# Sorting tokens for sixteen experts: from four-row groups of one tile to five-row groups of a pair of tiles

## The chip, the core and the metric

The kernel runs on one core of a Trainium2 chip. The metric is the device time of one execution, in microseconds (us). A time "before" or "after" is the median of several executions; one further execution of each kernel was profiled, and all durations below are from it.

## What is computed

`x` has shape (8, 64, 32, 32). A convolution-like block is added to it (a layer norm over channels, a projection to 16 channels, a Fourier filter, a projection back). Its result is read as 8192 tokens of 64 channels, and a mixture of experts is added:

```python
logits = einsum('bsd,de->bse', layernorm(t), gate_w) + gate_b   # 16 experts
top_probs, top_idx = top_k(softmax(logits), 2)                  # the best two of each token
dispatch = sum(one_hot(top_idx) * (top_probs / sum(top_probs))[..., None], axis=-2)
hidden = silu(einsum('bsd,edh->bseh', x, w1)) * einsum('bsd,edh->bseh', x, w2)
t = t + einsum('bseo,bse->bso', einsum('bseh,eho->bseo', hidden, w3), dispatch)
```

## The kernel before

The first 100 us (convolution block, gate logits of the first half) are the same in both kernels. The 8192 tokens are 64 tiles of 128 tokens, and two halves of 32 tiles (`HT`) that follow each other. Each half passes five stages.

1. **Route and sort.** VectorE picks the two best experts of each token (`route`) and works out each token's place in the tile, sorted by expert (`sort_places`). Each expert's tokens in a tile start at a multiple of `GRP` rows, so that a group of `GRP` rows belongs to one expert. For each tile VectorE builds a one-hot matrix in two instructions (`one_hots`, L1290 and L1292); TensorE multiplies by it (`sort_tile`, L872), once for each of the `GRP` rows of a group; ScalarE copies the sorted rows out of PSUM (`sorted_out`, L591 and L592); and GpSimd writes the tile's groups to `sorted_x` in HBM with one indirect transfer (`scatter`, L1479). TensorE also transposes the one-hots (`turn_hots`, L879) and ScalarE keeps them (`hott_out`, L599) for the way back.
2. **Load.** SyncE reads blocks of `GBLK` groups of one expert back (`load`), eight blocks (an octet) at a time. TensorE transposes them (L930), ScalarE copies them out (`tokens_out`, L618).
3. **Experts.** Four blocks are a quad `q`. For each quad TensorE runs the two up projections (`up`, L965 and L966, 16 matmuls, in high and low halves of float16), ScalarE the silu (`gate`, L624), VectorE the product (`product`, L1371), TensorE the down projection of quad `q - 2` (`down`, L978), ScalarE copies it out (`y_out`, L630) and SyncE stores it in `sorted_y` (`store_y`, L447). VectorE also copies each quad's weights to a fixed place (`fetch`, L1362), two quads ahead. L754 is a filler matmul that does no work.
4. **Return.** GpSimd gathers a tile's groups with one indirect transfer (`gather`, L1485). VectorE multiplies by the routing weights (`weigh`, L1378), ScalarE makes the high half (`high_part`, L636), VectorE the low half (`low_part`, L1384), and TensorE adds the rows back into token order (`back_to_tokens`, L992 to L1013).
5. **Result.** ScalarE copies out (`result`, L647) and SyncE stores.

The engines' order is written out by hand. The second half's sorting is spread over the first 19 quads of half 0 (`sorts_in`), and the first half's return over quads 4 to 21 of half 1 (`RET_START, RET_STEPS`). In half 1 a step of VectorE is `product(q)`, `fetch(q + 2)`, then for each tile `m` of the step `weigh(m)` and `low_part(m - 1)`. A step of TensorE is `up(q)`, `down(q - 2)`, an octet's transposes in every second step, and `back_to_tokens(m - BACK_LAG)`, with `BACK_LAG` 3. In half 1 the matmuls of the second up projection read their weights from `w_all` at an address in a register; the first reads the copy. The second half's return runs alone, after the last quad. 16 of its 32 transposed one-hots were kept; the others are built and transposed again there (`remade`).

```python
            def weigh(m):
                dve.wait_ge(gathered[m % YL_RING], 16 * (m // YL_RING + 1))
                ...
            def low_part(m):
                dve.wait_ge(yw_done, m + 1)
                dve.wait_ge(yhi_done, m + 1)
                ...
            def back_to_tokens(m):
                pe.wait_ge(ylo_done, m + 1)
```

Sizes follow from `GRP`: with 4, a tile has 76 groups (`TGROUPS`), a block 32 groups, a half 92 blocks and so 23 quads.

Of the kernel before, what the change touches and what calls it, by code (L numbers as in the profile page):

```python
# [10 lines left out]
I32 = mybir.dt.int32  # L11
# [24 lines left out]
GRP = 4  # L36
TGROUPS = (2 * P + E * (GRP - 1)) // GRP
TSLOTS = TGROUPS * GRP
GBLK = P // GRP
QUAD = 4  # L40
# [5 lines left out]
OROWS = OCT * P  # L46
# [18 lines left out]
HOTS = 6  # L65
SORT_RING = 8
# [3 lines left out]
PAST_AFTER, OWNERS_AFTER, ROUTE_AFTER = 8, 17, 14  # L70
COUNTS_AFTER, RANKS_AFTER, PLACES_AFTER = 24, 27, 29
UPFRONT, SORT_STEPS = 4, 19
FILLERS, HALF1_FILLED = 1, 6
EARLY_BASE = 3
KEPT = 16
XG_RING, YS_RING, YL_RING = 4, 8, 8
SPLIT_RING = 4
ACC_BANKS, HOTT_TAIL, OUT_BANKS = (4, 5), (0, 1), (2, 3)
ADD_LAG = 6
RET_START, RET_STEPS, BACK_LAG = 4, 18, 3  # L80
TURN = 4
RESULT_LAG = 5
OUT_AT = {2: 0, 5: 1, 8: 2, 11: 3}
# [52 lines left out]
def constant_tile():  # L136

    eye = np.eye(P)
    mean = np.kron(np.eye(2), np.full((C, C), 1.0 / C))
    rev = np.broadcast_to((E - np.arange(E))[None, :, None], (P, E, HT)).reshape(P, -1)  # L140
    lane = np.arange(P)[:, None]
# [22 lines left out]
def build(nc, x, w_in, w_out, bin_w, gate_w, gate_b, w1, w2, w3, t_const, t_perm, t_fwd, t_neg, t_inv, t_bins, out):  # L164
    ctx = ExitStack()
    with ctx:
# [3 lines left out]
        def sem(name):  # L170
# [41 lines left out]
        stepped_to = picked_space[0:TGROUPS, 0:E * HT]  # L212
        stepped = shared16[0:TGROUPS, after + 4 * PIX:after + 4 * PIX + 2 * E * HT].bitcast(F32)
# [9 lines left out]
        xg = w_raw16[:, 0:XG_RING * OROWS].rearrange("p (o n) -> p o n", n=OROWS)  # L223
# [48 lines left out]
        addr_f = sb("addr_f", [TGROUPS, HT])  # L272
        addr = sb("addr", [TGROUPS, HALVES, HT], I32)
        back_f, back = sb("back_f", [TGROUPS, HT]), sb("back", [TGROUPS, HALVES, HT], I32)
        hots = [tok[:, :, :, :].rearrange("p a t c -> p (a t c)").bitcast(F16)[:, r * TSLOTS:(r + 1) * TSLOTS].rearrange("p (g s) -> p g s", s=GRP)
                for r in range(HOTS)]
        sorted_t = [xs[:, :].bitcast(F16)[0:TGROUPS, r * BLK:(r + 1) * BLK] for r in range(SORT_RING)]
        yl = [xs[0:TGROUPS, COLS // 2 + r * GRP * C:COLS // 2 + (r + 1) * GRP * C] for r in range(YL_RING)]
        hott = [t[0:TGROUPS, r * BLK:(r + 1) * BLK].rearrange("g (s t) -> g s t", s=GRP)
                for t, n in ((xq.bitcast(F16), 16), (w_raw16[:, XG_RING * OROWS:], 12), (turned_space, 4)) for r in range(n)]  # L280
        kept_hott = [t[0:TGROUPS, r * BLK:(r + 1) * BLK].rearrange("g (s t) -> g s t", s=GRP)
                     for t, n in ((shared16, 8), (work[:, 4, :].bitcast(F16), 4), (picked_space.bitcast(F16), 4)) for r in range(n)]
        yw = [cand[:, :, :, :].rearrange("p k e t -> p (k e t)").bitcast(F32)[0:TGROUPS, r * GRP * C:(r + 1) * GRP * C].rearrange("g (s c) -> g s c", s=GRP)
              for r in range(2)]
        y_parts = [chosen[:, :, :, :, :].rearrange("p k j e t -> p (k j e t)")[0:TGROUPS, r * BLK:(r + 1) * BLK].rearrange("g (s a c) -> g s a c", s=GRP, a=2)
# [9 lines left out]
        sorted_y = [nc.dram_tensor(f"sorted_y{k}", (SLOT_BLOCKS * P, C), F32).ap() for k in range(HALVES)]  # L295
# [1234 lines left out]
```

## Time and profile before

| | |
|---|---|
| median of 3 runs | 378.61 us (377.3 to 378.87) |
| the profiled execution | 376.88 us |
| its span, first to last instruction | 374.8 us |
| busy: TensorE / VectorE / ScalarE / GpSimd | 298.6 / 268.9 / 221.5 / 179.5 us |
| mean granted clock of TensorE | 0.762 of 2.4 GHz |
| indirect transfers | 64 scatters and 64 gathers |

The profile gives for each instruction its start and duration, for each idle stretch what ended it, and TensorE's granted clock (1.0 is 2.4 GHz, 0.5 is 1.2 GHz). Matmuls overlap each other: their pace is the difference of two starts, not their duration. The five stages lie in time as follows: common start to 100.8, sorting of half 0 to 162.6, quads of half 0 to 233.7, quads of half 1 to 311.2, and from the first gather of half 1's return at 318.1 to the end.

### The profile page before, as it was taken

To read this page: it belongs to the slowest core of one execution; us is meant where nothing else is said; L and a number is where in the kernel's file an instruction comes from. 1 tells how busy PE (TensorE), PEld (TensorE's weight loads), DVE (VectorE), ACT (ScalarE), POOL (GpSimd) and SP (SyncE) were. 2 spreads that over 40 slices of the span, in tenths; PEclk is the share of its full clock that TensorE was granted. 3 is DMA by queue.
4 is the path that set the end of the run, shared out by engine and by line. 5 is a ranking of instruction groups with operands and counts; after the bars stand their busy time and mean duration, and the time that the engine had idled before them with its cause. 6 is when DMAs were issued, how large, how long until landed. Compare 5 with 4: busy or idle time off the path is not lost.

```text
span 374.8 us, 8710 instructions
## 1 busy us (share of the span) xinstructions
PE 298.6 (80%) x2802; PEld 251.6 (67%) x2802; DVE 268.9 (72%) x716; ACT 221.5 (59%) x484; POOL 179.5 (48%) x157
## 2 busy tenths in 40 slices
PE   4879567957476677469999998998878895799996
PEld 4737346855255554259998987888777784588884
DVE  1964574497999954959999967467878885883762
ACT  4878844562177675449898985455555552555431
POOL 2016263330088785445655650077865400887880
PEclk9959985555855568659999999898999996555555
DMA  7999900000012121242545454455544512233432
GB/s 222 338 260 385 387 24 0 2 2 0 0 45 53 50 56 35 65 118 47 137 117 139 114 133 90 99 138 142 132 106 107 128 37 53 50 103 87 111 79 70
DMA packets 55390, 39.89 MB, mean 106 GB/s; under 512 B 37660, under 2 KB 49692, under 8 KB 54708
## 3 DMA queue, kind: packets, MB, share of 16 engines
q1 hardware_dynamic: 42804, 29.25, 27.5%
q0 software_dynamic: 12384, 10.10, 11.3%
q8 instruction: 24, 0.39, 0.5%
q14 instruction: 18, 0.15, 0.1%
q10 hardware_dynamic: 160, 0.01, 0.0%
HBM read 20.08 MB, written 19.14 MB: 105 GB/s over the span
## 4 chain that ended last, share of the span: by engine, by line
PE 36%; DVE 26%; ACT 11%; issue 10%; DMA 8%; POOL 4%; SPq 2%; DVEq 1%; POOLq 0%; ACTq 0%
PE banks L978 7%; PE banks L872 4%; DMA w_raw<-in_L_ffn_w 4%; POOL xs L1485 4%; PE banks L966 4%; PE banks L965 4%; DVE tok L1292 4%; DMA xs<-sorted_y,back 3%; DVE cand L1378 3%; PE banks L879 3%; PE banks L930 3%; PE banks L1013 2%; PE banks L764 2%; ACT fold L624 2%; DVE work L1362 2%
## 5 line engine op out<-in xcount | busy, mean ns | idle before, releaser
L1479 POOL DMA_INDIRECT sorted_x<-xs,addr x64 | 75.7, 1183 | 67.4 <-ACT xs L591 36.5
L1485 POOL DMA_INDIRECT xs<-sorted_y,back x64 | 74.7, 1167 | 65.0 <-issue 53.6
L591 ACT CAST xs<-banks 76x512 f16<-76x512 f32 x64 | 37.2, 581 | 34.7 <-PE banks L872 34.5
L636 ACT CAST chosen<-cand 76x256 f16<-76x256 f32 x64 | 25.9, 405 | 49.6 <-DVE cand L1378 37.1
L978 PE MATMUL banks<-w_all,power 128*128 x368 | 51.4, 285 | 4.3 <-DVE power L1371 2.3
L872 PE MATMUL banks<-shared,tok 128*76 128x131 f16 x256 | 34.8, 274 | 23.9 <-ACT wcol L592 13.3
L978 PEld LDWEIGHTS banks<-w_all,power 128*128 128x128 f32 x368 | 47.0, 199 | 6.0 <-issue 5.6
L1371 DVE SCALAR_TENSOR_TENSOR power<-banks,fold 128x512 f32<-128x512 f32 x46 | 31.7, 688 | 25.2 <-ACT fold L624 21.7
L872 PEld LDWEIGHTS banks<-shared,tok 128*76 128x76 f16 x256 | 25.7, 167 | 31.1 <-DVE tok L1292 19.9
L1292 DVE SCALAR_TENSOR_TENSOR tok<-perm,local,tok 128x304 f16<-128x304 f16 x80 | 42.7, 534 | 2.8
L1362 DVE COPY work<-w_all 128x512 uint16 (+1 forms) x184 | 39.1, 282 | 6.6 <-issue 6.3
L879 PE MATMUL banks<-ident,tok 128*76 128x128 f16 x256 | 36.5, 286 | 4.5 <-DVE tok L1292 2.6
L965 PE MATMUL banks<-shared,work 128*128 128x128 f16 x276 | 37.3, 224 | 0.0
L966 PE MATMUL banks<-shared,work 128*128 128x128 f16 x276 | 37.3, 224 | 0.0
L1378 DVE TENSOR_TENSOR cand<-xs,w_loc 76x256 f32<-76x256 f32 x64 | 26.9, 420 | 9.7 <-DMA xs<-sorted_y,back 6.6
L879 PEld LDWEIGHTS banks<-ident,tok 128*76 128x76 f16 x256 | 28.4, 174 | 7.4 <-ACT scratch L599 4.0
L1384 DVE TENSOR_TENSOR chosen<-cand,chosen 76x256 f16<-76x256 f32 x64 | 26.7, 417 | 7.9 <-ACT chosen L636 7.9
L966 PEld LDWEIGHTS banks<-shared,work 128*128 128x128 f16 x276 | 27.8, 101 | 3.7 <-issue 0.6
L624 ACT ACTIVATE fold<-banks 128x512 f32<-128x512 f32 x46 | 27.4, 596 | 4.1 <-PE banks L966 3.6
L618 ACT COPY shared<-banks 128x1024 f16<-128x1024 f16 (+1 forms) x24 | 23.4, 974 | 8.1 <-PE banks L930 7.8
L1290 DVE TENSOR_SCALAR tok<-perm,local 128x304 f16<-128x304 f16 x80 | 25.3, 317 | 3.8 <-PE banks L879 3.8
L965 PEld LDWEIGHTS banks<-shared,work 128*128 128x128 f16 x276 | 27.7, 100 | 0.0
(200 smaller groups left out, 620.0 us busy)
## 6 DMA issues: line engine op xcount, KB each, us to landing
sorted_x<-zeros SPq DMA_DIRECT2D x2, 2944.0 KB, 30.4
w_raw<-sorted_x SPq DMA_DIRECT2D x22, 256.0 KB, 3.5
sorted_y<-filt SPq DMA_DIRECT2D x96, 32.0 KB
sorted_y<-enh SPq DMA_DIRECT2D x88, 32.0 KB
w_raw<-in_L_ffn_w SPq DMA_DIRECT2D x5, 512.0 KB, 16.1
xs<-in_x SPq DMA_DIRECT2D x8, 256.0 KB, 4.6
out<-cen_sq SPq DMA_DIRECT2D x8, 256.0 KB, 3.7
shared<-in_t_fwd SPq DMA_DIRECT2D x1, 1024.0 KB, 7.8
```

The costliest lines, as they stand in the source:

```text
L591: nc.scalar.copy(sorted_t[n % SORT_RING].rearrange("g (a b n) -> g a b n", a=2, b=2), sorted_rows[:, :, :, 0:2 * C]).then_inc(sorted_done, 1)
L624: nc.scalar.activation(gated[:, q % 2, :], bank[q % 2], ACT.Silu, scale=1.0 / WSCALE).then_inc(silu_done, 1)
L872: last = nc.tensor.matmul(banks[SORT_PAIR][0:TGROUPS, s // 2, at:at + ROW], hots[n % HOTS][:, :, s], rows[:, n, 0:ROW], start=True, stop=True)
L879: last = nc.tensor.transpose(target.bitcast(F16)[0:TGROUPS, s * P:(s + 1) * P], hots[use % HOTS][:, :, s], ident16[:, :])
L965: nc.tensor.matmul(dst, up_weights(k, i, b, a, experts), tokens[:, b, :, :], start=True, stop=False)
L966: last = nc.tensor.matmul(dst, up_weights(k, i, b, a + 1, experts), tokens[:, b, :, :], start=False, stop=True)
L978: last = nc.tensor.matmul(y_bank(q)[:, b * C:(b + 1) * C], hid[:, q % RING, b * P:(b + 1) * P], of_expert(experts[(q % NQ % 2) * QUAD + b] ...
L1292: nc.vector.scalar_tensor_tensor(hot, slot_iota, local[:, k, 0, t:t + 1], hot, ALU.is_equal, ALU.add).then_inc(hot_done, 1)
L1362: last = nc.vector.tensor_copy(fetched_w[:, (q % FETCH_RING) * QUAD + b, 0:parts_read * HID], w_all[:, bass.ds(fetching[o][(i % 2) * QUAD ...
L1378: nc.vector.tensor_tensor(yw[m % 2], yl[m % YL_RING].rearrange("g (s c) -> g s c", s=GRP), w_loc[:, k, t, :].unsqueeze(2).to_broadcast([TG ...
L1479: nc.gpsimd.indirect_dma_start(out=sorted_x[k].rearrange("(g s) c -> g (s c)", s=GRP), out_offset=bass.IndirectOffsetOnAxis(ap=addr[:, k, ...
L1485: nc.gpsimd.indirect_dma_start(out=yl[m % YL_RING], out_offset=None, in_=sorted_y[k].rearrange("(g s) c -> g (s c)", s=GRP), in_offset=bas ...
```

## The change

`GRP` becomes 5. A tile then has 64 groups, so that two tiles (a pair) fill 128 partitions: a half has 16 pairs (`HP`), and every sort, scatter, gather and return handles a pair. A block is 25 groups (125 rows), a half has 100 blocks and 25 quads. There are 32 scatters and 32 gathers, of 128 rows of 1280 bytes, in place of 64 and 64 of 76 rows of 1024 bytes. All 32 transposed pairs of one-hots are kept, so nothing is remade. The sort's PSUM pair is used as two halves in turn (rows 0 to 2, rows 3 and 4 of a group). `fetch` copies all four parts of the weights in half 1 too. `store_y` is one transfer of 125 partitions instead of four of 32, and `load` reads 100 partitions instead of 128. `weigh` works in place, on 128 partitions; `high_part` and `low_part` work on each tile's 64 partitions apart, into `y_parts`, which GpSimd zeroes once. `back_to_tokens` first adds the residual and the means, then waits, then runs 10 matmuls of 128 by 128. `BACK_LAG` becomes 1. The results of the first half go straight from PSUM, during half 1.

```diff
-GRP = 4
+GRP = 5
-RET_START, RET_STEPS, BACK_LAG = 4, 18, 3
+RET_START, RET_STEPS, BACK_LAG = 4, 18, 1
...
             def store_y(q):
                 k, i = q // NQ, q % NQ
-                rows = sorted_y[k][i * BLK:(i + 1) * BLK, :].rearrange("(b g s) c -> s g b c", b=QUAD, s=GRP)
                 sp.wait_ge(y_done, q + 1)
-                for s in range(GRP):
-                    sp.dma_start(rows[s], ys[q % YS_RING][s * GBLK:(s + 1) * GBLK, :].rearrange("g (b c) -> g b c", b=QUAD)).then_inc(y_stored[q % YS_RING], 16)
+                sp.dma_start(sorted_y[k][i * QW:(i + 1) * QW, :].rearrange("(b p) c -> p b c", p=BW),
+                             ys[q % YS_RING][0:BW, :].rearrange("p (b c) -> p b c", b=QUAD)).then_inc(y_stored[q % YS_RING], 16)
...
             def high_part(m):
+                act.wait_ge(parts_zero, 1)
                 act.wait_ge(yw_done, m + 1)
                 if m >= SPLIT_RING:
                     act.wait_ge(back_ps, m - SPLIT_RING + 1)
-                nc.scalar.copy(y_parts[m % SPLIT_RING][:, :, 0, :], yw[m % 2]).then_inc(yhi_done, 1)
+                for h in range(2):
+                    nc.scalar.copy(y_parts[m % SPLIT_RING][tile_half(h), :, 0, h, :], yl[m % YL_RING][tile_half(h), :, :]).then_inc(yhi_done, 1)
...
+            def sort_pair(n, a):
+                k, j = n // HP, n % HP
+                for h in range(2):
+                    pe.wait_ge(hot_done, 2 * n + h + 1)
+                if j == 0 and a == 0:
+                    pe.wait_ge(mean1_done, 1)
+                    pe.wait_ge(wt_done, k + 1)
                 if n >= 1:
-                    pe.wait_ge(wcol_done, n)
+                    pe.wait_ge(wcol_done, 2 * n + a - 1)
+                for s in rows_in(a):
+                    at = (s - rows_in(a)[0]) * ROW_STRIDE
+                    for h in range(2):
+                        hot = hots[n % HOTS][:, h * TSLOTS:(h + 1) * TSLOTS].rearrange("p (g s) -> p g s", s=GRP)
+                        last = nc.tensor.matmul(banks[SORT_PAIR][tile_half(h), a, at:at + ROW], hot[:, :, s], rows[:, 2 * n + h, 0:ROW], start=True, stop=True)
+                last.then_inc(sort_ps, 1)
...
             def back_to_tokens(m):
 
-                pe.wait_ge(ylo_done, m + 1)
...
+                n, u = m // BP, m % BP
+                sums = bank[ACC_BANKS[n % 2]][:, u * P:(u + 1) * P]
+                if u == 0 and n >= 2:
+                    pe.wait_ge(res_done, n - 1)
+                nc.tensor.matmul(sums, ct[:, m, 0:P], ident, start=True, stop=False)
+                for h in range(2):
+                    nc.tensor.matmul(sums[h * C:(h + 1) * C, :], both_parts[:, 2 * m + h:2 * m + h + 1].to_broadcast([P, C]), mean_rows[:, :],
+                                     start=False, stop=False)
+                pe.wait_ge(hott_done, m + 1)
+                pe.wait_ge(ylo_done, 2 * (m + 1))
                 for s in range(GRP):
                     for a in range(2):
-                        last = nc.tensor.matmul(acc[h * C:(h + 1) * C, u * P:(u + 1) * P], y_parts[m % SPLIT_RING][:, s, a, :], home[:, s, :],
-                                                start=False, stop=(s == GRP - 1 and a == 1))
+                        last = nc.tensor.matmul(sums, y_parts[m % SPLIT_RING][:, s, a, :, :], hott[m][:, s, :], start=False, stop=(s == GRP - 1 and a == 1))
                 last.then_inc(back_ps, 1)
...
             def return_step(m):
-                k, t = m // HT, m % HT
                 weigh(m)
-                if t >= 1:
+                if m >= 1:
                     low_part(m - 1)
```

TensorE in half 1, between two quads, before: the end of a down projection (L978), one tile's return (L992, L995) and the next up projection (L965). Bracketed are the semaphores that a row waits for.

```order
L978 MATMUL banks<-w_all,power 128x64
L992 MATMUL banks<-ident,mean_rows 128x128 [waits hott_done,ylo_done]
L995 MATMUL banks<-chosen,scratch 128x128 x4
L965 MATMUL banks<-shared,work 128x128 [waits silu_done,fetched,xt_done]
L966 MATMUL banks<-shared,work 128x128
```

The same place in the changed program, for a pair (L983, L985 and L991 are its return, L960 the next up projection):

```order
L973 MATMUL banks<-w_all,power 125x64
L983 MATMUL banks<-cst,ct 128x128
L985 MATMUL banks<-mean_rows,both_parts 64x128 x2
L991 MATMUL banks<-w_raw,xs 128x128 [waits ylo_done,hott_done]
L991 MATMUL banks<-w_raw,xs 128x128 x9
L960 MATMUL banks<-shared,work 128x125 [waits silu_done,fetched,xt_done]
```

The place of the return between `down` and the next `up` is the same; the wait for the low parts has moved behind the residual and means, and it is now for pair `m - 1` of the step, not for tile `m - 3`.

VectorE in half 1, one step before: the copies of weights (L1362, each with a row that sets its address), then `weigh` (L1378), `low_part` (L1384), the sums of four tiles (L1390, L1391), a second tile, and the next quad's product (L1371).

```order
L1362 COPY work<-w_all 128x256
L1378 TENSOR_TENSOR cand<-xs,w_loc 76x256 [waits ylo_done,gathered6]
L1384 TENSOR_TENSOR chosen<-cand,chosen 76x4x64 [waits yhi_done,yw_done]
L1390 TENSOR_TENSOR ct<-ct,banks 128x2x128 [waits back_ps]
L1391 TENSOR_TENSOR ct<-ct,banks 128x2x128 [waits dve_own]
L1378 TENSOR_TENSOR cand<-xs,w_loc 76x256 [waits ylo_done,gathered7]
L1384 TENSOR_TENSOR chosen<-cand,chosen 76x4x64 [waits yhi_done,yw_done]
L1371 SCALAR_TENSOR_TENSOR power<-banks,fold 128x512 [waits y_ps,h2_done,silu_done]
```

The changed program's step (L1315 copies weights, L1328 weighs pair `m`, L1335 makes the low parts of pair `m - 1`, L1324 is the next product):

```order
L1315 COPY work<-w_all 128x512
L1315 ISA
L1315 COPY work<-w_all 128x512
L1328 TENSOR_TENSOR xs<-xs,w_loc 128x320 [waits gathered3]
L1335 TENSOR_TENSOR xs<-xs 64x5x64 [waits yhi_done] x2
L1324 SCALAR_TENSOR_TENSOR power<-banks,fold 128x500 [waits y_ps,h2_done,silu_done]
```

The low parts that TensorE waits for in a step stand behind the four weight copies and `weigh` of the same step, which themselves stand behind that step's product.

## Rows read from the trace of the kernel before

**Rows 1.** Busy time by stretch: us, each engine's busy time (instructions), clock, DMA.

```profile
100.80:162.60 61.80, 40.63 (x306) 30.59 (x307) 50.41 (x124) 40.30 (x107) 41.22 (x35) 0.58 0.23 61
162.60:233.70 71.10, 66.98 (x836) 62.33 (x837) 59.32 (x180) 57.47 (x129) 34.50 (x30) 0.95 0.44 105
233.70:311.20 77.50, 66.14 (x795) 60.64 (x795) 55.61 (x184) 41.49 (x90) 36.78 (x32) 0.96 0.47 110
318.10:374.80 56.70, 50.45 (x395) 40.69 (x393) 34.96 (x91) 24.78 (x56) 37.94 (x32) 0.50 0.30 83
```

**Rows 2.** Chain that ended last, in the sorting of half 0: start, us, what.

```profile
130.30 0.65 PE banks L872 x4
130.97 0.45 ACT xs L591
131.45 0.17 ACT wcol L592
131.76 0.65 PE banks L872 x4
```

**Rows 3.** Timeline of VectorE, one tile's one-hots and the next's.

```profile
108.30 0.28 DVE L1290 TENSOR_SCALAR tok<-perm,local 128x304 f16<-128x304 f16 x1
109.07 0.29 DVE L1290 TENSOR_SCALAR tok<-perm,local 128x304 f16<-128x304 f16 x1
```

**Rows 4.** Timeline of VectorE in half 0: four weight copies, then a one-hot.

```profile
216.05 0.90 DVE L1362 COPY work<-w_all 128x512 uint16 x4 [0.25 <-issue]
216.87 0.29 DVE L1290 TENSOR_SCALAR tok<-perm,local 128x304 f16<-128x304 f16 x1
```

**Rows 5.** Timelines of TensorE, ScalarE and VectorE, early quads of half 1.

```profile
237.75 0.38 PE L754 MATMUL banks<-perm,ident 128*128 128x512 f16 x1
239.76 0.38 PE L754 MATMUL banks<-perm,ident 128*128 128x512 f16 x1
...
242.86 0.38 PE L754 MATMUL banks<-perm,ident 128*128 128x512 f16 x1
...
240.62 0.60 ACT L624 ACTIVATE fold<-banks 128x512 f32<-128x512 f32 x1 [0.28 <-PE banks L966]
...
241.25 0.69 DVE L1371 SCALAR_TENSOR_TENSOR power<-banks,fold 128x512 f32<-128x512 f32 x1 [0.46 <-ACT fold L624]
```

**Rows 6.** Timeline of TensorE in half 1: five matmuls lie between these two starts.

```profile
267.59 0.22 PE L992 MATMUL banks<-ident,mean_rows 128*128 128x128 f16 x1
...
267.87 0.22 PE L992 MATMUL banks<-ident,mean_rows 128*128 128x128 f16 x1
```

**Rows 7.** Groups of the page: busy us, mean ns of one, idle before.

```profile
L1479 POOL DMA_INDIRECT sorted_x<-xs,addr x64 | 75.7, 1183 | 67.4 <-ACT xs L591 36.5
L1485 POOL DMA_INDIRECT xs<-sorted_y,back x64 | 74.7, 1167 | 65.0 <-issue 53.6
...
L1378 DVE TENSOR_TENSOR cand<-xs,w_loc 76x256 f32<-76x256 f32 x64 | 26.9, 420 | 9.7 <-DMA xs<-sorted_y,back 6.6
```

**Rows 8.** TensorE by stretches of 2 us in half 1: busy time, granted clock, DMA.

```profile
256.00:258.00 2.00, 0.98 (x15) 1.00 0.52 118
258.00:260.00 2.00, 2.00 (x19) 0.50 0.36 72
```

**Rows 9.** End of the chain that ended last.

```profile
364.36 4.14 DMA xs<-sorted_y,back
...
369.33 0.79 PE banks L1007 x2
...
370.37 1.30 PE banks L1013 x16
```

**Rows 10.** Busy time by stretch, in half 0 and in half 1 with stores alone.

```profile
186.00:216.00 30.00, 29.40 (x383) 27.78 (x381) 27.89 (x81) 27.27 (x63) 17.38 (x15) 1.00 0.53 127
302.00:310.00 8.00, 7.00 (x83) 6.29 (x82) 6.58 (x20) 4.19 (x11) 0.00 (x0) 1.00 0.20 41
```

More of the change, by code:

```diff
@@ L278, in build @@
[L278 to L282, printed above, removed]
@@ L454, in _ @@
                     store_y(NQ * k + 2 * o + h)
+                    if k == 1 and 2 * o + h in STORE_AFTER:
+                        store(STORE_AFTER[2 * o + h])
                 if n + XG_RING < HALVES * OCTETS:
                     load(n + XG_RING)
-            for n in range(NBLK):
+            for n in range(len(STORE_AFTER), NBLK):
                 store(n)
@@ L868, in sort_tile @@
                 if n >= 1:
-                    pe.wait_ge(wcol_done, n)
-                for s in range(GRP):
-                    at = (s % 2) * ROW_STRIDE
-                    last = nc.tensor.matmul(banks[SORT_PAIR][0:TGROUPS, s // 2, at:at + ROW], hots[n % HOTS][:, :, s], rows[:, n, 0:ROW], start=True, stop=True)
-                last.then_inc(sort_ps, 1)
-            def turn_hots(use, target):
-                pe.wait_ge(hot_done, use + 1)
-                for s in range(GRP):
-                    last = nc.tensor.transpose(target.bitcast(F16)[0:TGROUPS, s * P:(s + 1) * P], hots[use % HOTS][:, :, s], ident16[:, :])
+                    pe.wait_ge(wcol_done, 2 * n + a - 1)
@@ new lines, in sort_places, with one_hots @@
+                step(nc.vector.scalar_tensor_tensor(back_f[:, :], addr_f[:, :], lane, bank[MISC_BANK][:, P:P + HT], ALU.add, ALU.add))
+                for h in range(2):
+                    nc.vector.tensor_copy(addr[tile_half(h), k, :], tiles_of(back_f, h)).then_inc(addr_done, 1)
+                for h in range(2):
+                    nc.vector.tensor_scalar(back[tile_half(h), k, :], tiles_of(back_f, h), SLOT_GROUPS - 1.0, None, ALU.min).then_inc(addr_done, 1)
+            def one_hots(n):
+                k, j = n // HP, n % HP
+                if n >= HOTS:
+                    dve.wait_ge(hott_ps, n - HOTS + 1)
+                hot = [hots[n % HOTS][:, h * TSLOTS:(h + 1) * TSLOTS] for h in range(2)]
+                for h in range(2):
+                    nc.vector.tensor_scalar(hot[h], slot_iota, local[:, k, 1, 2 * j + h:2 * j + h + 1], None, ALU.is_equal).then_inc(hot_second, 1)
+                for h in range(2):
+                    dve.wait_ge(hot_second, 2 * n + h + 1)
+                    nc.vector.scalar_tensor_tensor(hot[h], slot_iota, local[:, k, 0, 2 * j + h:2 * j + h + 1], hot[h], ALU.is_equal, ALU.add).then_inc(hot_done, 1)
@@ L1294, in experts_of_groups @@
             def experts_of_groups(k):
-                nc.vector.tensor_reduce(group_expert[:, k, :], stepped.rearrange("p (e t) -> p t e", e=E), AX_X, ALU.add)
+                step(nc.vector.tensor_reduce(group_of[:, :], stepped.rearrange("p (e t) -> p t e", e=E), AX_X, ALU.add))
+                for h in range(2):
+                    nc.vector.tensor_copy(group_expert[tile_half(h), k, :], tiles_of(group_of, h))
             def slot_weights(k):
```

453 lines of the change are left out of this document (183 added, 270 removed).

## The prediction

> **What bounds the kernel now.** I read the busy times by stretch first, then in each stretch the chain of waits or the timelines of the engines that wait for each other. No engine bounds the whole program: each stretch has its own limit.
>
> In the sorting of half 0, 61.8 us, no engine is busy throughout and TensorE's clock is mostly the lower one [rows 1]. The chain shows a closed circle of one tile: four sort matmuls, ScalarE's copies of the rows and of the weight columns, the next tile's four matmuls, 1.46 us from start to start [rows 2]. TensorE has one PSUM pair for it and waits until it is empty. VectorE alone would make a tile's one-hots in 0.77 us [rows 3].
>
> In half 0, TensorE, VectorE and ScalarE are all over 90% busy at the full clock in the 30 us from 186 to 216 [rows 10]. Nothing there can be added for nothing.
>
> In half 1, 77.5 us for 23 quads or 3.37 each, TensorE is 85% and VectorE 72% busy [rows 1]. The limit is order, not work.
>
> The last stretch, 56.7 us, holds half 1's return alone, at a clock of 0.50 [rows 1]. GpSimd issues a gather each 1.47 us (1.167 and a gap of 0.3) [rows 7]. From the first gather at 318.1 to the last at 364.36 [rows 1, 9] are 31 intervals of 1.49, so this pace sets the stretch. 10.4 us follow: landing, weighing, matmuls, result and store [rows 9].
>
> **The change part by part.**
>
> *Sorting of half 0.* The two PSUM halves in turn break the circle. A pair then costs each engine its own work. VectorE: twice 0.77, or 1.54 [rows 3]; 5% more columns, but two instructions no longer wait for their own results, so 1.5. ScalarE: copies of 1280 columns in place of 2048, about 1.4. TensorE at the lower clock: five transposes of 0.11 and ten sort matmuls of 64 output columns; a matmul of 128 columns takes 0.056 at full clock (five in 0.28 [rows 6]), so 0.11 at half, and the pair takes 1.65 if none of them overlap. I take 1.6 a pair, against 2.92. The first 14 tiles lie beside VectorE's routing of half 1 and give nothing. The other 18 take 26.3 now and nine pairs would take 14.4, which is 11.9 less. Of this I give back 3: the counts, ranks and places of half 1 stand among the last four pairs, and TensorE comes to them before VectorE is through with its one-hots. **−9 us**; bounds −4 (the routing's chain hides most) and −12.
>
> *Quads of half 0.* Each half has 25 quads, not 23. A quad without sorting takes 2.0 us, or 3.1 with an octet's transposes, so 2.55 in the mean (fillers at 237.75, 239.76, 242.86 [rows 5]). Now 71.1 us go to 23 quads [rows 1]. A quad with a pair will be held by VectorE: product 0.6, copies 0.82 [rows 4] and 0.13 for reading addresses, one-hots 1.5, so 3.05, which with three engines so full I round to 3.2. 14 such, 11 others at 2.3 to 2.5 and the slow first quads (71.1 less 19 at 3.05 and 4 at 2.3: 4) give 74. **+3**; bounds −3 and +7.
>
> *Quads of half 1.* This is where I expect the loss. In the new order, a step's low parts (pair `m - 1`) stand on VectorE behind its product, four copies and `weigh(m)`. TensorE waits for them before `up(q + 1)`, and the product of `q + 1` waits for that. So the engines close a circle in each step with a pair. From the start of `up`: silu 0.64 later (240.62 less 239.76 and 0.22 of filler), product 0.63 later, 0.6 of product [rows 5]; copies with addresses 0.95 [rows 4]; weighing and two low parts, each 0.42 by the row of 256 columns [rows 7] and 0.07 for 64 more, overlapping by 0.07 twice, 1.33; release 0.06; ten matmuls 0.56 [rows 6]. Sum 4.8 us. TensorE's other work (`down`, transposes, residual) lies in its shadow. Before, three tiles of lag kept the low parts a step ahead. There are 15 such steps. The other ten are five of 2.55 before the return, the first pair's at 3.2, one of 2.6 and three of 2.3, the last of which ends with its product, so two count. With 1.5 up to the first product: 72 + 12.8 + 3.2 + 2.6 + 4.6 + 1.5 = 96.7, against 77.5: +19. TensorE idles 1.7 of 4.8 us in it. Its clock fell at 258 after a stretch only half busy [rows 8], so I add 2 for such falls. **+21**; bounds: 0 if the circle does not close and VectorE or TensorE's own work of 3.1 decides, +34 if the lower clock stays (5.7 a step).
>
> The copies of all four parts cost VectorE 0.28 more a quad, which is in the circle. Their gain, no addresses in registers for the up projections, I put at nothing: TensorE does not wait for them in the circle.
>
> *The return of half 1.* 16 gathers for 32. The trace has none of 128 rows. If the cost is one of the instruction, the pace is 1.47; if it goes with rows, 1.47 × 128/76 = 2.5 at most. I take 1.7, nearer the first: scatters and gathers, which read and write different sides, cost nearly the same (1.183 and 1.167), so most of it looks like the instruction's own. Then 15 × 1.7 to the last gather, and behind it some 10.1 (half copies cost 0.9 more, the residual ahead of the wait saves 1.3): 35.6, against 56.7. But TensorE at the lower clock needs 0.8 for the residual [rows 9], 0.1 for the means and ten times 0.11, 2.0 a pair: 6.9 to its first matmul, 32 for 16 pairs, 3.1 behind, 42. Its clock may be up for part of it, since it would then work without a pause. I take 38.6 us. **−18**; bounds −25 (pace 1.47, full clock) and −9 (2.5).
>
> The four issues of the last store become one, which saves 1.3 us, and a longer landing takes it back. GpSimd's zeroing lies between its last scatter and first gather, where it idles. Storing three results in half 1 costs nothing: each waits for a result some quads old.
>
> *Sum.* −9 + 3 + 21 − 18 = −3, from the profiled 376.9 to 374. The median of the runs is 1.7 above that execution, so **376 us**.
>
> **The rivals.**
>
> *The forecast's mechanism*, gains at both ends and the circle in half 1, between 366 and 384: chance 0.50.
>
> *The circle does not close (faster).* If VectorE's low parts come so early that TensorE never waits, 15 steps cost 3.4 and not 4.8: 21 us less, 355. For it: TensorE's `down` and transposes fill 2 us of the wait. Against it: the rows put the low parts 4.2 us behind the start of `up`, and this decides from a lead of 1.4 on. 0.15.
>
> *The clock falls in half 1 (slower).* The same circle, with TensorE at 1.2 GHz: 0.45 more to the silu and 0.55 more for the return, 5.7 a step, 14 us more: 388. For it: the fall at 258. Against it: half-busy stretches elsewhere in half 1 kept the mean at 0.96 [rows 1]. 0.12.
>
> *Stores on few DMA engines (slower).* A store of 125 partitions has the same bytes as before, but may not spread as evenly. With stores alone, engines are 20% busy at 41 GB/s, so one full engine moves 13 GB/s in such rows; with loads and scatters beside them 15 [rows 10]. If only 5 of 16 engines carry a store of 128 KB, each is busy 2 us a quad with it, 0.85 with its part of loads on 10 engines and 0.5 with scatters, 3.3 in all, more than the 2.95 that a quad of half 0 takes: 8 us more, 384. Against it: eight store buffers and four load buffers take up waits. 0.13.
>
> The Trainium skill, "DMA: Bandwidth & Descriptors", section "Why a DMA increments its semaphore by 16 and not by 1", states this as a rule: a transfer uses the largest number of engines up to 16 that divides its slowest dimension, which it says gives 10 for 100 partitions. By it 125 gives 5. It would give 384 where even spreading gives 376, and no row here has a transfer of such a shape. By it the zero fill of `sorted_x`, also on 125 partitions, would take three times as long, into a part of the program in which nothing waits for it yet.
>
> *Gathers by rows (slower).* At 2.5 a gather, the last stretch gives back 9: 385. 0.10.
>
> **How the numbers follow.** The range from 361 to 392 holds the forecast's band, half of the faster case and most of the three slower ones, which leave out about 0.15 together. About 0.5% is what a measurement of this kernel can tell: 376.7 and 380.5. Faster: the 0.15 and two thirds of the forecast's 0.50, 0.48. Same: 0.12, all of it from the forecast's band. Slower: 0.35 from the last three rivals and 0.05 from the band's upper end, 0.40. Gains and losses of some 20 us nearly cancel, so the sign rests on which term I mis-sized.
>
> **What would show it.** In the profile of the changed kernel: sorts of half 0 at 1.6 us a pair, with quads starting near 153.5; 25 quads of half 0 in 74 us, with VectorE over 90% busy; steps of 4.8 us in half 1, with TensorE waiting for VectorE's low parts some 1.7 us in each of 15 steps; gathers each 1.7 us and a last stretch of 38 to 39. Steps of 3.4, a last stretch paced by 2.5, or long waits for loads and stores in half 0 would each prove a term wrong.

## The result, and the profile after

| | before | after |
|---|---|---|
| median of 4 runs each, us | 378.7 | 384.4 |
| profiled execution, us (its span) | 376.9 (374.8) | 383.7 (381.9) |
| granted clock, mean | 0.762 | 0.817 |

The ratio is 1.0145, with a 95% interval from 1.0114 to 1.0177: the changed kernel is slower by about 1.5%. The forecast was 376.0, faster by a little. Its range held the time, its sign was wrong. Below, a ratio leaves out an execution that took over 1.5% more than the fastest of its kernel, and a time is the median of all of them.

The stretches of the changed kernel, cut at the same events as [rows 1]: first sort matmuls, first token transposes, first `up` of half 1, last product, first gather of half 1's return. The columns are the same.

```profile
102.90:155.40 52.50, 30.01 (x304) 19.88 (x305) 47.63 (x129) 28.20 (x93) 20.52 (x18) 0.63 0.21 74
155.40:233.80 78.40, 74.22 (x955) 65.45 (x956) 58.63 (x187) 57.14 (x145) 17.91 (x17) 0.97 0.37 104
...
233.80:342.20 108.40, 82.15 (x935) 77.41 (x935) 56.16 (x163) 52.07 (x108) 15.26 (x16) 0.86 0.31 84
342.20:349.90 7.70, 2.19 (x19) 1.80 (x17) 0.67 (x1) 0.77 (x2) 0.00 (x0) 0.90 0.36 92
...
349.90:381.90 32.00, 21.05 (x234) 17.11 (x234) 23.05 (x50) 17.53 (x37) 16.83 (x16) 0.86 0.41 124
```

Set beside [rows 1], the terms of the sum come out so:

| stretch | forecast | measured |
|---|---|---|
| up to the first sort | 0 | +2.1 |
| sorting of half 0 (61.8 to 52.5) | −9 | −9.3 |
| quads of half 0 (71.1 to 78.4) | +3 | +7.3 |
| quads of half 1 (77.5 to 108.4) | +21 | +30.9 |
| last product to first gather (6.9 to 7.7) | 0 | +0.8 |
| return of half 1 (56.7 to 32.0) | −18 | −24.7 |
| sum | −3 | +7.1 |

Both large terms are of the kind that was forecast, and both are larger. Half 1 missed by 10 us and half 0 by 4; the return missed by 7 the other way. With half 1 as forecast and all else as measured, the sum would be −3.

**Half 1, step by step.** VectorE's timeline over two steps with a pair (start, us, what; in brackets the idle time before, and who ended it):

```profile
258.41 0.68 DVE L1324 SCALAR_TENSOR_TENSOR power<-banks,fold 128x500 f32<-128x500 f32 x1 [3.15 <-ACT fold L624]
259.01 0.89 DVE L1315 COPY work<-w_all 128x512 uint16 x4
259.81 0.48 DVE L1328 TENSOR_TENSOR xs<-xs,w_loc 128x320 f32<-128x320 f32 x1
260.22 1.00 DVE L1335 TENSOR_TENSOR xs<-xs 64x320 f16<-64x320 f32 x2
263.18 0.68 DVE L1324 SCALAR_TENSOR_TENSOR power<-banks,fold 128x500 f32<-128x500 f32 x1 [1.97 <-ACT fold L624]
264.17 0.90 DVE L1315 COPY work<-w_all 128x512 uint16 x4 [0.30 <-issue]
264.98 0.48 DVE L1328 TENSOR_TENSOR xs<-xs,w_loc 128x320 f32<-128x320 f32 x1
265.38 1.00 DVE L1335 TENSOR_TENSOR xs<-xs 64x320 f16<-64x320 f32 x2
269.53 0.68 DVE L1324 SCALAR_TENSOR_TENSOR power<-banks,fold 128x500 f32<-128x500 f32 x1 [3.15 <-ACT fold L624]
```

TensorE's matmuls of the return, which wait for the low parts, in the step before and in the same two steps, and ScalarE's silus behind them:

```profile
255.41 1.23 PE L991 MATMUL banks<-scratch,xs 128*128 128x128 f16 x10 [2.80 <-DVE xs L1335]
...
261.36 0.72 PE L991 MATMUL banks<-scratch,xs 128*128 128x128 f16 x10 [1.02 <-DVE xs L1335]
...
266.53 1.23 PE L991 MATMUL banks<-scratch,xs 128*128 128x128 f16 x10 [1.77 <-DVE xs L1335]
...
262.56 0.59 ACT L624 ACTIVATE fold<-banks 128x500 f32<-128x500 f32 x1 [1.24 <-PE banks L961]
...
268.63 0.59 ACT L624 ACTIVATE fold<-banks 128x500 f32<-128x500 f32 x1 [2.15 <-PE banks L961]
```

The first step is the circle of the forecast at full clock. From one product to the next: 0.60 of product, 0.80 of copies, 0.41 of weighing, 1.14 of low parts and release (TensorE starts at 261.36), 0.56 for ten matmuls, 0.64 to the silu, 0.62 to the product: 4.77, where 4.8 was forecast. In the second step the ten matmuls and the `up` run at 1.2 GHz: 1.02, 1.08 and 0.90 in those three places, 1.18 more. Another 0.39 goes to reading the addresses of a new octet before the copies. That makes 6.35. With and without the low clock and the reading, a step is 4.8, 5.2, 5.9 or 6.3 long. Twelve of the 15 steps in which TensorE returns a pair are within 0.1 of one of these, six of them at 5.9 or more; the other three take 5.0 to 5.4. Together they take 82.7 us, 5.5 each. In the first slow one, from 252 to 256, TensorE was busy 1.2 us of 4; its clock was 0.60 there and 0.54 in the next four:

```profile
252.00:256.00 4.00, 1.20 (x14) 0.97 (x12) 2.86 (x8) 2.16 (x6) 0.46 (x1) 0.60 0.47 129
256.00:260.00 4.00, 4.00 (x32) 3.98 (x30) 1.59 (x6) 0.66 (x2) 0.48 (x1) 0.54 0.17 44
```

### The profile page after: what moved, and what is told of

It is laid out like the page before. It is cut to its first block and busy times, and to the rows that moved or that the text cites. A ratio compares the mean times of both kernels' runs of the same rounds, so it can differ in the third digit from the quotient of the medians.

```text
span 381.9 us, 8236 instructions
## 1 busy us (share of the span) xinstructions
PE 280.9 (74%) x2886; PEld 236.0 (62%) x2886; DVE 252.4 (66%) x664; ACT 212.2 (56%) x486; POOL 99.6 (26%) x96
## 5 line engine op out<-in xcount | busy, mean ns | idle before, releaser
L1324 DVE SCALAR_TENSOR_TENSOR power<-banks,fold 128x500 f32<-128x500 f32 x50 | 33.8, 676 | 62.7 <-ACT fold L624 58.1
L1417 POOL DMA_INDIRECT xs<-sorted_y,back x32 | 32.1, 1003 | 115.0 <-DMA sorted_y<-filt 59.7
L1411 POOL DMA_INDIRECT sorted_x<-xs,addr x32 | 34.9, 1091 | 100.7 <-ACT xs L591 98.9
L961 PE MATMUL banks<-shared,work 128*128 128x125 f16 x400 | 56.6, 232 | 0.0
L960 PE MATMUL banks<-shared,work 128*128 128x125 f16 x400 | 56.5, 234 | 0.0
L973 PE MATMUL banks<-w_all,power 128*125 x400 | 56.1, 287 | 0.2 <-DVE power L1324 0.2
L1315 DVE COPY work<-w_all 128x512 uint16 x200 | 47.2, 298 | 9.0 <-issue 9.0
L973 PEld LDWEIGHTS banks<-w_all,power 128*125 128x125 f32 x400 | 51.4, 202 | 1.2 <-issue 0.3
L624 ACT ACTIVATE fold<-banks 128x500 f32<-128x500 f32 x50 | 29.9, 598 | 28.4 <-PE banks L961 27.9
L960 PEld LDWEIGHTS banks<-shared,work 128*128 128x128 f16 x400 | 42.3, 106 | 0.0
L871 PE MATMUL banks<-shared,tok 128*64 128x131 f16 x320 | 24.7, 284 | 19.5 <-DVE tok L1243 19.2
L1243 DVE SCALAR_TENSOR_TENSOR tok<-perm,local,tok 128x320 f16<-128x320 f16 x64 | 32.0, 539 | 0.0
L1335 DVE TENSOR_TENSOR xs<-xs 64x320 f16<-64x320 f32 x64 | 31.0, 484 | 1.0
L991 PE MATMUL banks<-scratch,xs 128*128 128x128 f16 x120 | 11.0, 253 | 18.2 <-DVE xs L1335 18.1
L1328 DVE TENSOR_TENSOR xs<-xs,w_loc 128x320 f32<-128x320 f32 x32 | 15.6, 488 | 11.3 <-DMA xs<-sorted_y,back 10.9
L991 PEld LDWEIGHTS banks<-scratch,xs 128*128 128x128 f16 x120 | 8.8, 113 | 19.5 <-issue 19.5
```

Source lines behind the costliest of these rows:

```text
L624: nc.scalar.activation(gated[:, q % 2, 0:QW], bank[q % 2][:, 0:QW], ACT.Silu, scale=1.0 / WSCALE).then_inc(silu_done, 1)
L871: last = nc.tensor.matmul(banks[SORT_PAIR][tile_half(h), a, at:at + ROW], hot[:, :, s], rows[:, 2 * n + h, 0:ROW], start=True, stop=True)
L960: nc.tensor.matmul(dst, up_weights(k, i, b, a, experts), tokens[:, b, :], start=True, stop=False)
L961: last = nc.tensor.matmul(dst, up_weights(k, i, b, a + 1, experts), tokens[:, b, :], start=False, stop=True)
L973: last = nc.tensor.matmul(y_bank(q)[0:BW, b * C:(b + 1) * C], hid[:, q % RING, b * BW:(b + 1) * BW], of_expert(experts[(q % NQ % 2) * QUAD ...
L1243: nc.vector.scalar_tensor_tensor(hot[h], slot_iota, local[:, k, 0, 2 * j + h:2 * j + h + 1], hot[h], ALU.is_equal, ALU.add).then_inc(hot_d ...
```

## The experiments

**1. A longer lag.** The circle needs the low parts of pair `m - 1` in the step that makes them. With a lag of 2, TensorE takes those that were written a step earlier.

```diff
-RET_START, RET_STEPS, BACK_LAG = 4, 18, 1
-RESULT_LAG = 2
+RET_START, RET_STEPS, BACK_LAG = 4, 18, 2
+RESULT_LAG = 3
```

> The changed kernel with BACK_LAG 2 (and RESULT_LAG 3, so that a result is asked for as late as before): TensorE does pair m - 2 where it did m - 1. Theory of the circle: the low parts of m - 2 were written a step earlier, so TensorE no longer waits 1.0 to 2.8 us a step for them, a step with a pair costs 3.5 to 3.9 us in place of 4.8 at full clock and 6.3 at the low one, and the low clock goes too because TensorE has no pauses: 20 to 28 us less, 356 to 364. Rival, the stretch is held by transfers (stores of 125 partitions, gathers behind them): the wait moves to the gathers and the time stays within 3 of 384. Rival, VectorE's work: steps of 4.4 or more, 376 or more.

Measured: 359.6 us, ratio to before 0.950 (0.946 to 0.953). From half 1's first product to its last it takes 82.4 us, against 106.9 in the changed kernel and 75.5 in the kernel before. Most steps with a pair alternate between 3.5 and 4.0, and the clock is 0.95 from 252 to 316. Two take 6.2 and 5.1; in the first of them TensorE waited 1.4 us for ScalarE and 1.1 for nothing that the profile names, and its clock was 0.50 from 282 to 288. So the circle was the cause of the loss: opening it gave back 25 us, where the rival of transfers had the time stay within 3.

**2. The same circle, shortened.** The lag stays at 1, but in half 1 VectorE weighs and writes the low parts ahead of its copies.

```diff
                     product(q)
+                    if k == 1:
+                        if i == 0:
+                            dve.wait_ge(wloc_done, HALVES)
+                        for m in pairs_in(i, RET_START, RET_STEPS):
+                            return_step(m)
                     if q + FETCH_AHEAD < HALVES * NQ:
                         fetch(q + FETCH_AHEAD)
...
-                    else:
-                        if i == 0:
-                            dve.wait_ge(wloc_done, HALVES)
-                        for m in pairs_in(i, RET_START, RET_STEPS):
-                            return_step(m)
```

> The changed kernel with VectorE's order turned in half 1: product, weighing and low parts, then the four copies. Theory of the circle: the 0.9 us of copies leave it, so each of 15 steps costs 3.9 us and not 4.8 at full clock: 13 less; where the lower clock goes away too, up to 9 more: 362 to 371. Rival, the copies were needed just as soon (TensorE then waits for them): within 3 of 384. Rival of transfers: no change either.

Measured: 360.3 us, ratio 0.952 (0.948 to 0.956). The timeline of one step, VectorE and TensorE:

```profile
263.47 0.68 DVE L1324 SCALAR_TENSOR_TENSOR power<-banks,fold 128x500 f32<-128x500 f32 x1 [0.97 <-ACT fold L624]
...
264.06 0.48 DVE L1328 TENSOR_TENSOR xs<-xs,w_loc 128x320 f32<-128x320 f32 x1
...
264.46 1.00 DVE L1335 TENSOR_TENSOR xs<-xs 64x320 f16<-64x320 f32 x2
...
265.49 0.97 DVE L1315 COPY work<-w_all 128x512 uint16 x4
265.61 0.72 PE L991 MATMUL banks<-scratch,xs 128*128 128x128 f16 x10 [1.02 <-DVE xs L1335]
...
269.56 0.72 PE L991 MATMUL banks<-scratch,xs 128*128 128x128 f16 x10 [0.56 <-DVE xs L1335]
```

The circle is still closed: TensorE waits for the low parts in 14 of the 15 steps, mostly 0.56 and 1.02 in turn and twice 1.35 and 1.48. But 13 of the steps are 3.95 or 3.96 long, 0.8 less than 4.77, the copies. And none is at the low clock: the granted clock is 1.00 from 252 to 316. So waits of 0.4 to 1.5 in steps of 4.0 kept the clock here, and waits of 1.0 to 2.8 in the changed kernel did not always.

**3. Fewer copies.** One part of the change is undone in half 1: `fetch` copies 256 columns in place of 512, and `up` reads w2's weights from `w_all` with addresses in registers.

```diff
-                return fetched_w[:, ((NQ * k + i) % FETCH_RING) * QUAD + b, a * HID:(a + 1) * HID].bitcast(F16)
+                if k == 0 or a < 2:
+                    return fetched_w[:, ((NQ * k + i) % FETCH_RING) * QUAD + b, a * HID:(a + 1) * HID].bitcast(F16)
+                return of_expert(experts[(i % 2) * QUAD + b], a, HID).bitcast(F16)
...
+                width = (4 if k == 0 else 2) * HID
...
```

> The changed kernel with one part of the change undone: in half 1 VectorE copies only the weights of w1, and w2's up matmuls read w_all through registers. Theory of the circle: four copies take 0.45 us less in it, 24 quads, 15 in the circle: 7 less, 377, if registers cost TensorE nothing. Rival, the addresses in registers cost TensorE time (half a microsecond a quad): within 3 of 384 or up to 6 slower. If VectorE's copies are not in the limit at all: no change.

Measured: 379.9 us, ratio 1.002 (0.998 to 1.006), 4.4 less than the changed kernel; half 1 takes 103.7 from product to product, 3.3 less. Its ten executions lie between 375.6 and 382.2. The direction is the circle's; the size is about half to two thirds of the 7 us that it gives.

**4 and 5. The clock.** First a filler matmul ahead of every `up`; then four of them in a step with a pair, ahead of the wait for the low parts.

```diff
-FILLERS, HALF1_FILLED = 1, 6
+FILLERS, HALF1_FILLED = 1, 25
```

> The changed kernel with HALF1_FILLED 25: a filler matmul of 512 columns ahead of every up, in half 1 too. It costs 0.22 us at full clock and stands in the circle: 19 quads, 4 more. Theory that part of the loss is the clock: with fewer half-idle stretches the nine steps of 6.3 us become 5.0, 12 less, net 8 less: 376. Rival, the clock falls all the same, since one filler fills little of 1.0 to 1.8 idle: 4 to 7 slower, 388 to 391.

```diff
                         if m >= BACK_LAG:
+                            pe.wait_ge(silu_done, q)
+                            stay_warm(4, bank[(q + 1) % 2])
                             back_to_tokens(m - BACK_LAG)
```

> The changed kernel with four filler matmuls of 512 columns (0.22 us each at full clock) issued in each step of half 1 with a pair, ahead of the wait for the low parts, so that they fill the pause and not the circle. Theory that the pauses of 1.0 to 1.8 us cost the clock, and that six of the 15 steps were 1.4 us longer for it: all 15 at 4.8 to 5.2, 6 to 10 us less, 374 to 378. Rival, the clock falls all the same: the fillers at the low clock take 1.7 us, and the time is 384 or more.

Measured: 388.9 (ratio 1.019, 1.013 to 1.025) and 375.5 (0.992, 0.989 to 0.996). The first kernel's executions took 385.0, 387.0, 390.7 and 394.2, and the profile is of the third; the changed kernel's took 383.7 to 384.9. TensorE in half 1 by stretches, first with a filler ahead of every `up`, then the changed kernel, then with four in the pause (columns as in [rows 1]):

```profile
252.00:340.00 88.00, 66.26 (x632) 59.68 (x633) 40.80 (x118) 36.82 (x76) 9.41 (x10) 0.77 0.25 69
```

```profile
252.00:340.00 88.00, 64.00 (x697) 60.31 (x694) 45.76 (x131) 40.54 (x85) 9.45 (x10) 0.83 0.27 73
```

```profile
252.00:333.00 81.00, 65.70 (x766) 56.29 (x766) 45.95 (x131) 41.57 (x87) 9.45 (x10) 0.98 0.30 81
```

The filler ahead of `up` stands behind the wait: it leaves the pause, and it is in the circle, whose shortest steps are 4.98 and not 4.77. The clock did not go up. It was 0.77 here against 0.83, but over whole executions it was 0.81 to 0.83 against 0.80 to 0.82, so that it went down is not shown. The expectation of 8 us less was wrong, and its rival, 4 to 7 more, came true. Four fillers in the pause cost the circle nothing. The clock is 0.98, and 12 of the 15 steps are at 4.77 or 5.17; one of 5.4 reads its addresses for longer, and the first two, 5.6 and 4.9, have the one fall of the clock that is left (0.50 from 258 to 260, behind a wait of 2.2). Together the 15 take 75.4 us and not 82.7. So the low clock cost the changed kernel at least 7 us in these steps.

**6. The lag alone, in the kernel before.**

```diff
-RET_START, RET_STEPS, BACK_LAG = 4, 18, 3
+RET_START, RET_STEPS, BACK_LAG = 4, 18, 1
```

> The kernel before with BACK_LAG 1 in place of 3 and nothing else. Theory that the lag alone closes the circle: product 0.6, copies 0.82, weighing and low parts of two tiles, release, eight matmuls, up and silu make 4.8 us a step in place of 3.37: 15 to 25 us more than 378.7, 394 to 404, all of it in half 1. Rival, the circle needs the pairs (128 rows weighed and split at once) and does not close on single tiles: within 3 of 378.7.

Measured: 416.7 us, ratio 1.096 (1.087 to 1.104), 38 more than before. Half 1 takes 112.5 from product to product and not 75.5, and between 240 and 350 TensorE waits for low parts 23 times, 17.0 us in all. Its row shows what came on top of the 15 to 25 us that were expected:

```profile
250.00:348.00 98.00, 80.85 (x625) 74.23 (x626) 49.36 (x157) 34.95 (x75) 32.33 (x29) 0.56 0.30 69
```

The clock is 0.56, where half 1 before had 0.96 [rows 1]: here the circle and the low clock come together in most steps. The circle does not need the pairs: the one number `BACK_LAG` closes it.

**7. Stores over more DMA engines.** A store of 125 partitions becomes one of 112 and one of 13.

```diff
-                sp.dma_start(sorted_y[k][i * QW:(i + 1) * QW, :].rearrange("(b p) c -> p b c", p=BW),
-                             ys[q % YS_RING][0:BW, :].rearrange("p (b c) -> p b c", b=QUAD)).then_inc(y_stored[q % YS_RING], 16)
+                for part in (slice(0, 112), slice(112, BW)):
+                    sp.dma_start(sorted_y[k][i * QW:(i + 1) * QW, :].rearrange("(b p) c -> p b c", p=BW)[part],
+                                 ys[q % YS_RING][part, :].rearrange("p (b c) -> p b c", b=QUAD)).then_inc(y_stored[q % YS_RING], 16)
...
```

> The changed kernel with each store of a quad's results in two transfers, one of 112 partitions and one of 13, in place of one of 125. Rival of the prediction (one transfer of 125 partitions goes over few DMA engines and its lateness holds quads or gathers): 3 to 8 us less than 384.4, most of it in half 0 (78.4 us) and in the landing of the last store, 4.7 us. Theory that the stores are hidden: within 2 of 384.4, with the landing of the last store alone shorter by up to 2 us.

Measured: 382.2 us, ratio 1.013 (1.007 to 1.019), whose interval overlaps that of the changed kernel. The last store in the chain that ended last, in the changed kernel and with the split:

```profile
344.59 4.61 DMA sorted_y<-filt
```

```profile
343.91 1.72 DMA sorted_y<-filt
```

This landing is 2.9 us shorter, and the last stretch waits for it. Half 0 is not shorter: 71.1 us from first to last product, against 71.0. The rival was right that such a store lands late and wrong on what it would hold up.

**8. What a gather costs.** An extra gather of 64 rows goes into spare buffers ahead of each gather of 128.

```diff
+                if m >= 3:
+                    pool.wait_ge(gathered[(m - 3) % YL_RING], 32 * ((m - 3) // YL_RING + 1))
+                nc.gpsimd.indirect_dma_start(
+                    out=again[m % 3], out_offset=None, in_=sorted_y[k].rearrange("(g s) c -> g (s c)", s=GRP),
+                    in_offset=bass.IndirectOffsetOnAxis(ap=back[tile_half(0), k, j:j + 1], axis=0)).then_inc(gathered[m % YL_RING], 16)
...
```

> The changed kernel with an extra gather of 64 rows into spare buffers ahead of each gather of 128 rows; the output is the same. If a gather costs by its rows, the extra one takes 0.5 us of GpSimd where the other takes 1.0; if it costs by the instruction, both take 0.9 to 1.1. The last stretch then has two instructions a pair: with rows 2.1 us a pair and 10 us more than 32.0, by the instruction 2.6 a pair and 18 us more.

Measured: 403.6 us in a single run. GpSimd's timeline in the last stretch, extra gathers (L1420) and the others (L1423):

```profile
353.39 0.90 POOL L1420 DMA_INDIRECT chosen<-sorted_y,back  x1 [0.30 <-issue]
354.60 0.95 POOL L1423 DMA_INDIRECT xs<-sorted_y,back  x1 [0.30 <-issue]
355.86 0.90 POOL L1420 DMA_INDIRECT chosen<-sorted_y,back  x1 [0.30 <-issue]
```

64 rows take 0.90 and 128 rows 0.95; over the 16 of each in this stretch the means are 0.97 and 0.99. The cost is the instruction's. The stretch from first gather to end is 50.9 us and not 32.0, 18.9 more where 18 were expected.

**9 to 12. A version that beats both.** Lag 2 and the early low parts together; then without fillers as well; then with the split stores; then with w2's weights read through registers again.

The edit of the second step:

```diff
-FILLERS, HALF1_FILLED = 1, 6
+FILLERS, HALF1_FILLED = 0, 6
```

> Both measures together: BACK_LAG 2, and VectorE weighs and writes the low parts ahead of its copies. With either alone half 1 took 3.7 to 4.0 us a step. If each took away another part of the circle, the sum is a step of 3.5, TensorE's own work, and 4 to 8 us less than either: 352 to 356. Rival, the circle is open with either and another one holds both at 3.5 to 4.0 (product, weighing, ScalarE's high parts, the next silu): within 3 of 360.

> The same with FILLERS 0: no filler matmul of 0.39 us ahead of the up projections of half 0 and of the first six quads of half 1. Theory that TensorE's own work holds the quads of half 0 (busy 29.9 of 30.0 us from 186 to 216): 31 fillers of 0.22 to 0.39 go, 6 to 11 less than with them. Rival, they fill only what TensorE would wait for VectorE's products (the forecast's view of half 0): no change, or slower where the clock falls without them.

> BACK_LAG 2, low parts ahead of the copies, no fillers, and each store of results in two transfers, of 112 and of 13 partitions. In the changed kernel the split took the landing of the last store from 4.6 to 1.7 us. If that is all that the stores cost: 3 less than 348.8, 346. Rival, with steps of 2.9 us the slow stores now hold back more than the last one: 5 or more less, under 344. Rival, two issues a quad cost what they save: 348 to 350.

> The same kernel, and in half 1 VectorE copies only w1's weights, w2's up matmuls reading w_all through registers as in the kernel before. Theory that VectorE's own work holds the open steps (product 0.6, weighing 0.4, low parts 0.95, copies 0.95: 2.9): they fall to 2.45, 15 of them, 7 to 10 us less. Rival, TensorE's own work holds them (and the reading of addresses adds to it): no gain, or up to 8 us more.

| kernel | median, us | ratio to before (95%) | half 1, first to last product | clock there |
|---|---|---|---|---|
| both | 350.5 | 0.925 (0.923 to 0.927) | 71.7 | 1.00 |
| and no fillers | 348.8 | 0.919 (0.916 to 0.923) | 73.3 | 0.97 |
| and split stores | 341.5 | 0.901 (0.896 to 0.906) | 71.8 | 0.97 |
| and half the copies | 346.4 | 0.915 (0.911 to 0.919) | 75.7 | 0.98 |

Together they take eight of the 15 steps with a pair in 2.8 to 2.9, where each alone took 3.5 to 4.0, so the expected floor of 3.5 for TensorE was too high. To leave the fillers out gave 1.7 us, where 6 to 11 were expected. In half 1 of the third of these kernels TensorE hardly pauses any more, and in the fourth it pauses more although VectorE has less to do:

```profile
252.00:302.00 50.00, 48.77 (x668) 45.77 (x665) 44.66 (x129) 38.90 (x83) 9.45 (x10) 1.00 0.50 126
```

```profile
252.00:302.00 50.00, 46.51 (x624) 42.94 (x623) 37.54 (x118) 35.89 (x77) 8.47 (x9) 1.00 0.47 117
```

With the circle open VectorE's work does not decide, and undoing part of the copies costs 4.9 us where with the circle closed it had gained 4.4. The same edit has either sign. TensorE waits 3.4 us in this stretch ahead of its token transposes and not 1.1, for nothing that the profile names; so what makes the steps longer stays open.

The split stores gave 7.3 us here and not 3. The landing of the last store accounts for 2.9 (4.6 to 1.7 again). Half 0 was 3.6 shorter from first to last product, and most of that is one place: without the split TensorE waited 1.97 us before the token transposes at 169.9, for nothing that the profile names, and ran at 0.57 for the next 4 us. Whether a late transfer was behind it is open, since one profile of each kernel shows it.

## Why the prediction was wrong

**Sorting, −9: right.** VectorE makes the one-hots of a pair, two instructions of each kind, and they set the pace:

```profile
109.85 0.99 DVE L1243 SCALAR_TENSOR_TENSOR tok<-perm,local,tok 128x320 f16<-128x320 f16 x2
111.27 0.99 DVE L1243 SCALAR_TENSOR_TENSOR tok<-perm,local,tok 128x320 f16<-128x320 f16 x2
112.62 1.00 DVE L1243 SCALAR_TENSOR_TENSOR tok<-perm,local,tok 128x320 f16<-128x320 f16 x2
```

1.35 to 1.42 a pair where 1.6 was taken; the stretch is no shorter than forecast for it, since the routing of half 1 lies in between. The circle of one tile [rows 2] is gone.

**Half 1, +21: the step that failed by its size.** "4.8 us a step, 15 steps, 72, and 2 for falls of the clock" measured 82.7. The plain step was right: 4.77, in which the weighing and low parts take 1.55 with their release and not 1.39, and the copies 0.80 and not 0.95. With the clock nearly always up the 15 steps are 75.4 (experiment 5), 3.4 more than 72. The addresses of a new octet make up about that much, 0.4 to 0.6 in each of eight steps, where the forecast had 0.13 in every step. The low clock is the other 7.2, where 2 was set. This is the term that failed most. The trace of before had shown one fall [rows 8]; the rival that the clock stays low throughout was worked out at 5.7 a step and given 0.12. What came was in between, six steps of fifteen at about 6.25. A step at the low clock costs 1.18 more. The rival had 0.55 for the return and 0.45 to the silu, 1.0 together, though it wrote 5.7 for the step; the rows have 0.46 and 0.44, and 0.28 from the silu to the product, which it left out. A forecast that says that TensorE will pause 1.7 in each of 15 steps has to price the clock in the main sum. The rest of the half missed by 1. That the time came out within 2.3% of the forecast is in part luck, since the return's miss of 7 hid most of this one.

**Half 0, +3: 4 too small.** From the first product to the twentieth there are 19 steps, 14 with a pair, in 58.6 us, where 14 at 3.2 and five at 2.3 would be 56.3. The last steps and the way into half 1 take 15.3 where 13.8 was meant, one of them 5.1 us long, and the start takes 4.5 and not 4. The steps with a pair were right, 3.2 in the mean. Those without one were not: four of the five took 2.75 and the first 3.2, where 2.3 was taken. The prediction said that VectorE holds half 0, "over 90% busy". It is not. Here is the row of the same 30 us as [rows 10], and what VectorE waited for in all of half 0 (us in total, times, longest):

```profile
186.00:216.00 30.00, 29.90 (x386) 26.31 (x387) 22.32 (x71) 24.02 (x65) 7.71 (x8) 1.00 0.43 119
```

```profile
DVE power L1324 <- ACT fold L624: 9.2, 12, 1.7
DVE power L1324 <- PE banks L961: 4.5, 1, 4.5
DVE work L1315 <- issue: 4.3, 8, 0.8
```

VectorE is 74% busy and TensorE always; VectorE waits for silus, and these for TensorE. Without fillers (experiment 10) four quads of this stretch take 12.24 and not 12.88 (experiment 9), 0.16 a quad less, of the 0.22 that a filler takes at full clock. So TensorE's work holds at least part of half 0. How much of the 7.3 it is no run tells. It is not the stores: with the split ones half 0 takes as long (experiment 7).

**The return, −18: right in kind, 6.7 too small.** The pace is 1.44 a pair and not 1.7, and TensorE's clock is 0.86 and not 0.50. The gathers held it once, when VectorE waited 0.91 us for the fifth to land. The timeline of that wait and of one pair, VectorE and TensorE:

```profile
359.49 0.49 DVE L1328 TENSOR_TENSOR xs<-xs,w_loc 128x320 f32<-128x320 f32 x1 [0.91 <-DMA xs<-sorted_y,back]
...
365.32 0.49 DVE L1328 TENSOR_TENSOR xs<-xs,w_loc 128x320 f32<-128x320 f32 x1
...
365.43 0.72 PE L991 MATMUL banks<-shared,xs 128*128 128x128 f16 x10 [0.27 <-DVE xs L1335]
365.73 1.00 DVE L1335 TENSOR_TENSOR xs<-xs 64x320 f16<-64x320 f32 x2
...
366.76 0.49 DVE L1328 TENSOR_TENSOR xs<-xs,w_loc 128x320 f32<-128x320 f32 x1
```

VectorE's weighing and low parts take 1.44 without another pause, and TensorE waits 0.27 for them in most pairs. The forecast put a gather between 1.47 and 2.5 us apart from the next and left out that it could be less than before: the 16 gathers of this stretch take 0.94 to 1.14, 1.05 in the mean, and with 0.30 of gap that is 1.35.

**The start, +2.1: not foreseen.** The first sort waits for the one-hots of two tiles, 1.54 and not 0.91, and the addresses are written by four instructions in 0.81 and not by two in 0.18. That is 1.2; the other 0.9 lies earlier. The twelve kernels with the changed sort began it between 101.9 and 104.5, so that much is within what they differ by.

**The rivals.** The circle closed, so "it does not close" was wrong. The low clock was the nearest rival. Stores on few engines: the changed kernel's zero fill, on 125 partitions, runs at a DMA share of 0.33, about 5 engines of 16, as this row shows, and nothing waits for it.

```profile
50.00:85.00 35.00, 24.46 (x242) 21.63 (x240) 23.40 (x42) 18.82 (x32) 15.39 (x16) 0.57 0.33 119
```

The Trainium skill, "DMA: Bandwidth & Descriptors", section "Why a DMA increments its semaphore by 16 and not by 1", states that a transfer uses the largest number of engines up to 16 that divides its slowest dimension; for 125 partitions we work out 5 from it. The trace agrees, with 0.33 of 16 at 119 GB/s. The landing of a store fits it too, 4.6 us for 125 partitions and 1.7 for 112 and 13, though no view tells how many engines carry a store. Gathers by rows: refuted by experiment 8.

## What to carry to other kernels

Where one engine's late product is consumed in the same step by another that goes first in the next, a lag of one closes a circle through all of them. Walk it from one product to the next and add it up before a ring or a lag is made shorter to save space: here one number cost 25 us, and the pair of lag and order gave 34 back. A pause of TensorE in a circle can cost twice, once by itself and once by the clock. Four filler matmuls put into the pause gave the clock back; one put behind it did not, and made the circle longer. And an edit that frees an engine can be worth something of either sign, so measure it again when what bounds the step has moved.

## What the runs showed of the hardware

A gather of 64 rows occupied GpSimd for 0.90 us and one of 128 rows for 0.95 beside it, 1.00 in the mean of the changed kernel's 32, while one of 76 rows had taken 1.167 in the mean [rows 7]; fewer rows were not cheaper, and why 76 cost more than 128 no run tells. Pauses of TensorE of 0.4 to 1.5 us, one in each step of 4.0, left its clock at 1.00 over 64 us (experiment 2). Pauses of 1.0 to 2.8 in longer steps of the changed kernel let it fall in six steps of fifteen. It fell after one of 1.8, with 0.65 granted from 300 to 302 and 0.50 from 302 to 304, and stayed at 1.00 after another of 1.8. The ten matmuls behind the two pauses:

```profile
300.89 1.23 PE L991 MATMUL banks<-scratch,xs 128*128 128x128 f16 x10 [1.83 <-DVE xs L1335]
...
318.23 0.72 PE L991 MATMUL banks<-scratch,xs 128*128 128x128 f16 x10 [1.77 <-DVE xs L1335]
```

Splitting one store into 112 and 13 partitions cut its landing from 4.6 to 1.7 us with the same bytes.
